# A fused transformer pair on one core: input rows kept for the residual, loads and gathers reordered, last bias laid into the bank

## What is computed

```python
x = x + _L0_xattn_ref(_layernorm(x), ctx_1024, Wq, Wkv)          # 16 heads of 16, context of 120 rows
x = x + _L0_ffn_ref(_layernorm(x), W1, b1, W2, b2, gate_W, shared_W, shared_b, gamma, beta)
x = x + _L1_xattn_ref(_layernorm(x), ctx_1024, ctx_1024, mask, Wq1, Wk1, Wv1)   # one head, masked
x = x + _L1_ffn_ref(_layernorm(x), weight, bias)

def _L0_ffn_ref(...):
    probs = softmax(flat @ gate_W)            # top 2 of 8 experts, weights normalised -> combine
    out = 0.5 * gelu(flat @ shared_W + shared_b)
    for e in range(8):
        out = out + combine[:, e:e+1] * (gelu(flat @ W1[e] + b1[e]) @ W2[e] + b2[e])   # hidden 1024
    return layernorm(out) * gamma + beta

def _L1_ffn_ref(x, weight, bias):
    # rows and weights quantised to FP6 e2m3 in blocks of 32 with a scale each
    return xd @ wd.T + bias
```

## Time and profile before

| | |
|---|---|
| time, 3 runs | 1034.13 us median (1027.02 to 1041.34) |
| the profiled execution | 1036.61 us, span 1034.9 us |
| PE busy | 944.5 us (91% of the span) |
| DVE, ACT, POOL busy | 532.5, 509.8, 512.5 us |
| attention, expert phase, second phase, about | 0 to 329, 329 to 859, 859 to 1035 us |

### The profile page before, as it was taken

How to read it: one execution, slowest core, us unless ns; L and a number is a source line. 1 busy time by engine, 2 the same in 40 slices (tenths; PEclk the granted TensorE clock), 3 DMA queues, 4 the chain that set the end, 5 groups by cost and what they waited for, 6 DMA issues and landing times.

```text
span 1034.9 us, 22048 instructions
## 1 busy us (share of the span) xinstructions
PE 944.5 (91%) x7131; PEld 805.1 (78%) x7131; DVE 532.5 (51%) x1300; ACT 509.8 (49%) x1294; POOL 512.5 (50%) x675
## 2 busy tenths in 40 slices
PE   6999998899847996989999999999999999798776
PEld 4777776667636994979999999999999998586553
DVE  4787887789654351354232322223232223899972
ACT  4778776677534551323333333333333334577663
POOL 2443434566444135485554344344444432588883
PEclk9999999999888996999999999999999999999998
DMA  4354454544533355143332221222212226522201
GB/s 142 98 159 154 141 182 103 151 127 140 150 94 127 108 151 111 11 37 54 49 62 42 41 42 28 40 34 35 42 32 41 34 35 168 148 92 93 92 32 41
DMA packets 90735, 89.58 MB, mean 87 GB/s; under 512 B 19808, under 2 KB 85792, under 8 KB 90496
## 3 DMA queue, kind: packets, MB, share of 16 engines
q1 hardware_dynamic: 74944, 69.48, 22.8%
q0 software_dynamic: 15680, 18.69, 12.1%
HBM read 56.74 MB, written 31.39 MB: 85 GB/s over the span
## 4 chain that ended last, share of the span: by engine, by line
PE 68%; DVE 9%; DMA 8%; issue 4%; ACT 4%; POOL 3%; SPq 3%; another core or an unknown queue 1%; DVEq 0%; POOLq 0%; ACTq 0%
PE b_H L1562 24%; PE b_Y L1583 23%; DMA a_xres<-in_x 4%; PE a_T L934 4%; PE a_O L889 3%; PE a_O L948 3%; PE a_S L914 2%; DVE c_x_bn L2023 2%; DMA ffn_rows<-b_y,b_slots 2%; PE b_xT L1551 1%; PE a_M L983 1%; ACT c_xn L2145 1%; ACT c_probs L2190 1%; DVE c_centred L2036 1%; PE a_M L960 1%
## 5 line engine op out<-in xcount | busy, mean ns | idle before, releaser
L1732 ACT ACTIVATE b_hiddenT<-b_H,b_b 128x128 f32<-128x128 f32 x568 | 162.2, 370 | 338.4 <-PE b_H L1562 276.9
L1562 PEld LDWEIGHTS b_H<-b_rowsT,b_w 128*128 128x128 f32 x2272 | 269.6, 195 | 20.7 <-issue 10.1
L1562 PE MATMUL b_H<-b_rowsT,b_w 128*128 128x128 f32 x2272 | 272.2, 278 | 13.9 <-ACT b_rowsT L1739 6.0
L1583 PE MATMUL b_Y<-w_sb,b_hiddenT 128*128 x1136 | 260.3, 382 | 1.5 <-issue 1.3
L1583 PEld LDWEIGHTS b_Y<-w_sb,b_hiddenT 128*128 128x128 f32 x1136 | 212.1, 192 | 29.1 <-issue 2.8
L1500 POOL DMA_INDIRECT ffn_rows<-b_y,b_slots x71 | 137.6, 1938 | 190.1 <-DVE b_y L1667 124.7
L1663 DVE TENSOR_TENSOR b_y<-b_Y,b_b 128x256 f32<-128x256 f32 x71 | 30.2, 425 | 319.7 <-PE b_Y L1583 254.8
L1489 POOL DMA_INDIRECT b_rows<-xn_rows,b_slots x71 | 78.0, 1099 | 72.7 <-PE b_xT L1551 45.6
L1650 DVE COPY b_w<-w_sb 128x2048 f32 x71 | 87.5, 1233 | 39.9 <-issue 36.1
L1234 ACT COPY a_probsT<-a_T 120x512 f32<-120x512 f32 x128 | 74.9, 585 | 51.5 <-PE a_T L934 44.1
L934 PE MATMUL a_T<-ident,a_probs 128*120 128x128 f32 x512 | 79.6, 284 | 21.3 <-ACT a_probs L1226 21.2
(11 more groups left out here) (227 smaller groups left out, 1304.1 us busy)
## 6 DMA issues: line engine op xcount, KB each, us to landing
w_sb<-in_L_ffn_W SPq DMA_DIRECT2D x32, 512.0 KB
a_xin<-in_x SPq DMA_DIRECT2D x16, 256.0 KB
a_xres<-in_x SPq DMA_DIRECT2D x32, 128.0 KB
x_rows<-a_x SPq DMA_DIRECT2D x32, 128.0 KB, 1.7
xn_rows<-a_xn SPq DMA_DIRECT2D x32, 128.0 KB
shared_rows<-a_shared SPq DMA_DIRECT2D x32, 128.0 KB
b_spare<-shared_rows SPq DMA_DIRECT2D x16, 256.0 KB, 3.0
ffn_rows<-b_spare SPq DMA_DIRECT2D x16, 256.0 KB
```

Of the source, the lines that this page charges most:

```text
L1562: j = pe.matmul(H_ps[i][:, c * P:(c + 1) * P], w1c[i][:, k * HID + c * P:k * HID + (c + 1) * P], xT[:, k * P:(k + 1) * P], start=(k == 0), ...
L1583: j = pe.matmul(y_ps[i][:, 0:D], hT[i][:, c * P:(c + 1) * P], w2_sb[:, bass.ds(e * (HB * D) + c * D, D)], start=(c == 0), stop=(c == HB - 1))
L1732: j = act.activation(hT[i][:, c * P:(c + 1) * P], H_ps[i][:, c * P:(c + 1) * P], ACT.Gelu, bias=b1c[i][:, c:c + 1])
```

## The change

- **Input rows kept.** `xin` becomes a ring of four batches. Two of the places are the memory of the gathered rows (`lent`, named `b_rows` in the trace), which the expert phase uses later. The normalised rows get a buffer of their own, `a_xn`. `load_residual` and its 32 loads go; `residual` reads the ring. `load_x` waits for the transposes of one batch earlier and for the residual adds of four batches earlier. `stats1` has a new wait on POOL's inverse deviation, and `normalise_x` on PE's transposes.
- **SP's order.** `load_expert_weights(b + 2)` in place of `(b)`. `slots(0)` and `slots(1)` with `load_b2` come ahead of the other stores of cycles 14 and 15, not behind them. The chunk ring has six places, and six chunk loads are issued in cycles 11 to 13.
- **POOL's order.** The gather of slot tile 0 in cycle 15 moves from ahead of three puts and a residual add to behind them.
- **DVE's order.** `tile_weights(1)` moves ahead of the last tile's sums and statistics.
- **Memory.** `KEPT_Y` is 11 in place of 12, and the block scales' scratch of the weight preparation lies in the sixth chunk place. The routing's fill pattern lies in `b_spare`.
- **Second phase.** `add_bias` goes. ACT's `lay_bias` copies the bias into `f_ps` after `keep_result`, and `start_result` adds `x4` onto it with `start=False`. One more matmul at the phase's start sets the bank once.

```diff
-CHUNK_RING = 5
+CHUNK_RING = 6
...
-        xin = sb("a_xin", [P, 2, D])
-        xn = xin
+        xn = sb("a_xn", [P, 2, D])
...
-        xres = [sb(f"a_xres{u}", [P, D]) for u in range(2)]
+        XR = 4
+        xin = ([lent[:, 2 * i:2 * i + 2, :] for i in range(2)]
+               + [sb(f"a_xin{i}", [P, 2, D]) for i in range(2, XR)])
...
             def load_x(b):
                 if not batch(b):
                     return
-                ge(sp, s_xnT_p, b)
-                sp.dma_start(xin[:], x_b[b]).then_inc(s_xin, 16)
+                ge(sp, s_xnT_p, b - 1)
+                ge(sp, s_x2, 2 * (b - XR) + 2)
+                sp.dma_start(xin[b % XR][:], x_b[b]).then_inc(s_xin[b % 2], 16)
...
-            def load_residual(t):
-                if not tile(t):
-                    return
-                ge(sp, s_x2, t - 1)
-                sp.dma_start(xres[t % 2][:], x_t[t * P:(t + 1) * P, :]
-                             ).then_inc(s_xres[t % 2], 16)
...
                 load_x(b + 2)
-                load_residual(t - 1)
                 store_x2(t - 2)
                 load_ctx(b + 2)
                 if b == CYCLES[0]:
                     load_weights()
-                load_expert_weights(b)
-                load_residual(t)
+                load_expert_weights(b + 2)
+                if b == B - 2:
+                    starts["slots"](sp, 0)
+                if b == B - 1:
+                    starts["load_b2"](sp)
+                    starts["slots"](sp, 1)
                 store_shared(t - 3)
...
-                for c in {B - 4: (0, 1), B - 3: (2, 3), B - 2: (4,)}.get(b, ()):
+                for c in {B - 5: (0, 1), B - 4: (2, 3), B - 3: (4, 5)}.get(b, ()):
                     starts["load_chunk"](sp, c)
...
                 pool.wait_ge(s_att, t + 1)
-                pool.wait_ge(s_xres[t % 2], 16 * (t // 2) + 16)
-                pool.tensor_tensor(x2[t % 2][:], x2[t % 2][:], xres[t % 2][:], ALU.add
+                pool.wait_ge(s_xin[t // 2 % 2], 16 * (t // 4) + 16)
+                pool.tensor_tensor(x2[t % 2][:], x2[t % 2][:], xin[t // 2 % XR][:, t % 2, :], ALU.add
                                    ).then_inc(s_x2, 1)
...
-                if b == B - 1:
-                    starts["gather"](pool, 0)
                 put_some(b, 3)
...
                 inverse_std1(b + 2)
+                if b == B - 1:
+                    pool.wait_ge(s_x2, TILES - 4)
+                    starts["gather"](pool, 0)
...
-                dve.wait_ge(s_xin, 16 * b + 16)
+                dve.wait_ge(s_xin[b % 2], 16 * (b // 2) + 16)
+                ge(dve, s_r1, 3 * b)
...
             normalise2(t - 1)
+            starts["weights"](dve, 1)
             over_sums(t)
             stats2(t)
-            starts["weights"](dve, 1)
...
-        KEPT_Y = FIRST_ADD + 3
+        KEPT_Y = FIRST_ADD + 2
...
-                pool.wait_ge(s_x4, n + 1)
-                ge(pool, s_f_p, n - 1)
-                pool.tensor_tensor(x4b[n % 2][:], x4[n % 2][:],
-                                   fb[:].unsqueeze(1).broadcast_to(T2), ALU.add
-                                   ).then_inc(s_x4b, 1)
...
+            def lay_bias(n):
+                if not exists(n):
+                    return
+                if n == 0:
+                    act.wait_ge(second["s_vec"], 32)
+                    act.wait_ge(s_fb, 1)
+                ge(act, s_o, n)
+                act.copy(f_ps[:], fb[:].unsqueeze(1).broadcast_to(T2)).then_inc(s_fb, 1)
...
                 keep_result(c - 2)
+                lay_bias(c - 1)
...
-                pe.wait_ge(s_x4b, n + 1)
-                ge(pe, s_o, n)
+                pe.wait_ge(s_x4, n + 1)
+                pe.wait_ge(s_fb, n + 2)
                 pe.matmul(f_ps[:].rearrange("p u d -> p (u d)"), ident[:],
-                          x4b[n % 2][:].rearrange("p u d -> p (u d)"),
-                          start=True, stop=False, skip_group_check=True)
+                          x4[n % 2][:].rearrange("p u d -> p (u d)"),
+                          start=False, stop=False, skip_group_check=True)
```

More of the change, by code:

```diff
@@ L559, in attention_phase @@
         s_vinit = sem("a_vaug_set")
-        s_xin = sem("a_xin_loaded")
+        s_xin = [sem(f"a_xin{i}_loaded") for i in range(2)]
         s_ctx = sem("a_ctx_loaded")
-        s_xres = [sem(f"a_xres{u}_loaded") for u in range(2)]
         s_st1 = sem("a_ln1_stats")
@@ L1255, in normalise1 @@
                 act.wait_ge(s_r1, 3 * b + 3)
+                ge(act, s_xnT_p, b)
                 for v in range(2):
-                    i = act.activation(xn[:, v, :], xin[:, v, :], ACT.Identity, bias=nb1[:, v:v + 1],
+                    i = act.activation(xn[:, v, :], xin[b % XR][:, v, :], ACT.Identity, bias=nb1[:, v:v + 1],
                                        scale=rstd1[:, v:v + 1])
@@ L1349, in expert_phase @@
         vq, mg = wq, wk
-        am = sb("b_amax", [P, 2 * NB])
-        sc = sb("b_scale", [P, 2 * NB])
-        rsc = sb("b_rscale", [P, 2 * NB])
+        am, sc, rsc = (spare[:, (CHUNK_RING - 1) * CHUNK + i * 2 * NB:
+                             (CHUNK_RING - 1) * CHUNK + (i + 1) * 2 * NB] for i in range(3))
         H_ps = [ps(f"b_H{i}", [P, HID]) for i in range(2)]
@@ L2355, in tensor @@
                 pe.wait_ge(s, value)
+            pe.matmul(f_ps[:].rearrange("p u d -> p (u d)"), ident[:],
+                      wdT[:].rearrange("p k d -> p (k d)"), start=True, stop=True,
+                      skip_group_check=True).then_inc(s_fb, 1)
             for c in CYCLES:
```

36 lines of the change are left out of this document (14 added, 22 removed).

## The result

The changed kernel took **996.43 us** as a median of 4 runs (995.59 to 998.38), the kernel before 1035.49 beside it. The ratio is 0.9632 (95% interval 0.9562 to 0.9701), 3.7% faster. The profiled execution of the changed kernel took 995.59 us, with a span of 993.8 us: 41.1 less than the profiled one of before.

What follows compares the result with a forecast made beforehand. Bound: PE's chain, stretched in the attention by late residual-row DMA. 16.8 + 1.0 + 17.3 + 3.6 - 0.5 - 1.0 = 37.2 saved, less 3.7 leaves 33.5; 1036.6 to 1003.1, less 2.5 towards the median, rounded to 1000 us (985 to 1015).

Steps and rivals of the forecast that it cites:

- The six cycles: Attention cycles 9 to 14: without late residual rows they fall from 117.85 us to a 101.0 floor, 16.8 saved.
- The earlier cycles: Attention cycles ahead of cycle 9: already near the floor, 1.0 us saved for all of them.
- The end: End of the attention: five waits or slow pieces go, together 17.3 us saved, less 0.5 for slot loads ahead of stores.
- (a): Attention's end: POOL's first gather no longer holds up a residual add and slots are asked for earlier; 7.5 us saved.
- (c): Attention's end: the last projection, slowed by a fallen clock, runs at 2.4 GHz without the gaps; 1.8 us saved.
- (d): Attention's end: the last residual load goes and DVE's copy of the second tile's weights comes first; 2.9 us saved.
- (e): Attention's end: the matmul group at 329.00 took 5.42 us, a later tile's 3.73; 1.7 saved at full clock.
- (b): Attention's end: DVE's first copy of expert weights waits less, as the weights start two cycles earlier; 3.4 us saved.
- The start: Kernel's start: 1 MB of expert weights is queued ahead of the second batch's rows; 1 us of cost, 0 to 6.3.
- The second phase: Second phase: POOL's bias addition goes, so DVE's scale is no longer held; 14 times 0.26, 3.6 us saved, 0 to 4.5.
- The experts: Expert phase: the change touches nothing visible there; stalls may differ by a fifth, 8 us, either way.
- The first: Rival: DVE and POOL, not the residual, set the attention's pace; 17.65 us per cycle, 1013 in all; chance 0.12.

Runs made afterwards that it cites:

- e1: Changed kernel with the 32 residual loads back and the input ring only two batches deep; 1017.31 us median.
- e9: Changed kernel run again without any edit, in the third set of runs; 981.75 us median beside 1008.19 for the kernel before.
- e11: Changed kernel without the 32 puts of the attention, so the first half of the rows does not reach the experts; 981.29 us median.
- e7: Changed kernel without the 32 puts of the expert phase, so the second half of the rows does not reach the experts; 981.72 us median.
- e6: Changed kernel with only the gather of slot tile 0 and the slot loads with second bias at their old places; 1013.04 us median.
- e5: Changed kernel's input ring and memory moves; weight cycles, order at the attention's end and POOL's bias addition as in the kernel before; 1023.89 us median.
- e10: Changed kernel with only DVE's copy of the second tile's weights back behind the last sums and statistics; 983.77 us median.
- e4: Changed kernel with the attention's end in the old order: gather, slots with second bias, and second copy of weights back; 1012.28 us median.
- e3: Changed kernel with the expert weights loaded in their old cycles; 1007.13 us median.
- e2: Changed kernel with POOL adding the last bias again and no bias copy by ScalarE; 1009.88 us median.
- e12: Changed kernel with 12 y buffers, a chunk ring of five, old chunk-load cycles and the scales' scratch in its own memory; 980.96 us median.

## Why the prediction was right, step by step

The forecast was 1000 us (985 to 1015), and 996.43 was measured. It was right, and the steps beneath it were right to different degrees. That it came so close is in part luck. The two traces differ by 41.1 us, and the sum had 33.5 for them. Of the difference 5.4 us in the experts' stretch and 2.3 until the last result has landed are no edit's, as far as the runs show. Without them 33.4 are left, and there 1.1 more than forecast in the earlier cycles makes up for 1.2 less in the six cycles and the end.

Two sums in it do not come out. A tenth of what the six cycles and the end save is 3.4 us; 3.7 is a tenth of all 37.2. And 8 us either way with 0 to 4.5 in the second phase give 992 to 1012 around 1000.6, and 988 with the full 37.2, not 985. The measured time lies within either.

**The six cycles: 16.8 forecast, 13.1 in the first trace, with the floor of 101.0 as its foundation.** The mechanism held as written: the adds' waits on the DMA are gone, and come back with the loads (e1). The floor was no wish: e9 ran the six cycles in 101.4 us and e11 in 100.7, where the cycle with the ten extra groups took 17.08, 0.36 and not 0.7 over the others. What kept the first trace at 104.7 is no more than the tenth that the sum took off for whatever shows next. The forecast had ruled the puts out, since one cycle with puts ran at 16.72; but four of the six stay above the floor with no add waiting on a DMA. That the puts stretch them is not shown: e7 shows it for the expert phase alone, and for the attention it is argued from e9, in which both stretches shrink together.

**The earlier cycles: 1.0 forecast, 2.1 found.** All kernels with the ring have 133.9 us there, to the tenth, and e1 has 135.5.

**The end: 17.3 less 0.5 of cost forecast, 15.6 found.** (a) The gather's wait: 7.5 forecast, 7.0 by e6. (c) The slow projection: 1.8 forecast, 1.7 in the line itself (3.62 to 1.89), and it is at 1.89 with the ring alone (e5). (d) The second copy: 2.9 forecast, 2.3 and 2.6 by e10 and e4 less e6. (e) The first full group: 1.7 forecast, 5.42 to 3.73 (3.81 with the ring alone). Step by step along the kernels the end reads 1.9 for the ring (e5), 4.1 for the weights (e4), 2.6 for the copy (e6) and 7.0 for gather and slots. (b) The weights: 3.4 forecast, and the wait did fall, by 2.7 us. But the step gave the wrong cause for part of it: "The weights now start two cycles earlier" brings 0.2 at the end with the new order (e3) and 4.1 with the old one (e5 against e4). It is a wait that two edits each remove nearly whole, and the forecast had named one.

**The start: 1.0 of cost forecast, 1.0 found,** and nothing can be made of it, since the start varies by 2 us between executions with the same loads.

**The second phase: 3.6 forecast for the bias, 2.3 found against e2, 3.5 against before.** The size per batch was right, 0.26 us forecast and 0.25 found. What failed is the count, "14 times": nine periods gained it, five did not. Of the 5.9 in the first trace 2.3 is the wait for the last result, and 1.2 lies in long periods that the profiled execution of before had near its end (8.28 and 8.86 us, where e2 has 8.28 and 7.76). Whether these belong to the bias is open: periods over 8.1 us stand only in the three kernels with POOL's addition. That DVE is held by POOL stands on e2's line: 401 ns as a mean with POOL's addition, 174 without. By the Trainium skill (page "SBUF — State Buffer", section "Who interferes with whom") the two share a port pair under an exclusive lock, and the trace agrees.

**The experts: nothing forecast, with 8 us either way for the stalls; 5.4 faster in the first trace.** The width was too narrow for what these stalls do. Between executions of the same program the stretch was 514.1 and 500.5 us, and without puts 496.6. "The change touches nothing there that I can see" holds where it was tried: e12 puts the rings back and the stretch does not move, in the set in which the stalls were small.

**The rivals.** The first, that the next wait takes the place, is out: it asked for 17.65 us per cycle, and e9 has 101.4 for six. The first trace alone would not have said so, since its 104.7 lies nearer to the rival's 105.9 than to 101.0; there the end speaks, with 15.6 saved where the rival had 10. The second, the bias copy in PE's way, is out: PE waited 1.9 us for it in 16 batches, where the rival wanted 9.6. The third, stores that land late, is out: no wait on a store of `x_rows` is in the changed kernel's list of waits. Of what was to show, one thing did not: the granted clock at the attention's end is 0.86 from 265 to 290 us, not near 1, though from 290 us on it is 1.00, where 300:325 of before had 0.73. PE was busy only 19.29 of 24.61 us in this window; the gaps shrank and did not vanish.

**Where the forecast could have gone wrong.** It added the parts. One pair does not add: the early weights and the new order each remove most of DVE's wait for the first weights (4.63 us with neither, 1.96 with the new order, 1.25 with the early weights). Other parts do: at the end the ring is worth 1.9 us alone and 2.3 with all else changed. In the six cycles it is worth 6.3 alone and 14.3 to 17.5 with all else, but between single executions from different sets, so whether the parts add there is open. The forecast was made for all edits together, along one timeline, with each wait asked what else ends beside it, and so the sum of the end came out nearly right even where a part was booked to the wrong edit.

## What to carry to other kernels

Price a bundle of edits along one timeline of the whole, wait by wait, and not edit by edit: waits that two edits each remove count once, and a wait that is covered by another is worth nothing until the other goes. Where a load only fetches again what was on chip, its lateness can be removed by keeping the rows, and the cycles with no late load give the floor that the rest can reach (16.72 us here, reached by four of the six in e9). When an engine's operation is longer than elsewhere and ends with another engine's, here within 50 ns, suspect that it was held; moving the other work away tests it, and here gave back 0.25 us in nine of 15 periods. And run the changed kernel in every set of experiments: without it beside them, a difference of 10 us between two sets can't be told from that of an edit.

## What the runs showed of the hardware that was not expected

- POOL's indirect stores of small payloads can go with stalls of other engines. Without 32 of them PE was busy 94.83 of 95 us, with them 89.00 on the same chip and 84.19 beside the result; a single stall held ACT for 11.92 us with its input there.
- How dear they are differs between chips or times, which these runs cannot tell apart: the same program took 996.43 us and 981.75 us as medians, and the kernel before 1035.49 and 1008.19. The gain was 39 us in the one and 26 in the other. That part of what is saved is waits behind such stores would explain the difference; no run shows it.
- A DVE tensor_scalar of 128x16 takes 0.17 us alone and 0.43 when POOL is in an addition of 128x512 at its start.
